# A round trip of queries and keys through DRAM, laid out by chunk and stack row

## The reference

```python
x = x + 0.5 * ffn(layernorm(x))      # gate and up 256 -> 2048, tanh-gelu(gate) * up, down 2048 -> 256
x = x + attention(layernorm(x))      # qkv = x @ w_project.T; softmax(q k / 4, causal) @ v; @ w_out.T
x = x + 0.5 * ffn(layernorm(x))
```

## Time and profile before

| | us |
|---|---|
| median of 3 runs | 1058.31 (1054.94 to 1059.23) |
| the profiled execution | 1055.69 |
| its span in the trace | 1053.6 |
| TensorE (PE) busy | 948.1 (90%) |
| VectorE (DVE) busy | 621.1 (59%) |
| ScalarE (ACT) busy | 469.9 (45%) |
| GpSimd (POOL) busy | 232.7 (22%) |
| DMA engines | 20.26 MB moved, 21803 packets |

### The profile page before, as it was taken

The page is one execution under the profiler, slowest core; times in us unless marked ns, Lnnn a source line. Parts: engine busy times, 40 slices in busy tenths (PEclk is TensorE's granted clock), DMA queues, the critical chain, the costliest instruction groups (busy, mean ns, idle before and its releaser), DMA issues.

```text
span 1053.6 us, 16739 instructions
## 1 busy us (share of the span) xinstructions
PE 948.1 (90%) x6726; PEld 410.9 (39%) x6726; DVE 621.1 (59%) x1008; ACT 469.9 (45%) x634; POOL 232.7 (22%) x261
## 2 busy tenths in 40 slices
PE   2879996998999999899999998999998685999998
PEld 1435553543444535224544222434322121255544
DVE  6986244654864688545788455688757574062221
ACT  2224142133227331796330998532298382933240
POOL 3744273033200440002330000042000000034140
PEclk9889998999999999999999999999999696999999
DMA  7000032006000060000230000000000000000000
GB/s 246 1 0 2 1 69 33 2 1 100 1 2 2 1 101 1 2 2 2 63 40 7 15 2 2 1 1 1 21 2 2 1 1 2 1 1 1 21 1 20
DMA packets 21803, 20.26 MB, mean 19 GB/s; under 512 B 4064, under 2 KB 21472, under 8 KB 21728
## 3 DMA queue, kind: packets, MB, share of 16 engines
q1 hardware_dynamic: 18528, 16.06, 7.9%
q10 hardware_dynamic: 3200, 3.15, 0.9%
HBM read 12.78 MB, written 6.29 MB: 18 GB/s over the span
## 4 chain that ended last, share of the span: by engine, by line
PE 74%; DVE 9%; ACT 6%; issue 5%; DMA 3%; SPq 1%; POOL 1%; ACTq 0%; DVEq 0%; POOLq 0%
PE ps L1102 11%; PE ps L1073 11%; PE ps L1074 10%; PE ps L1075 10%; PE ps L1251 10%; PE ps L1206 7%; PE ps L1103 5%; ACT inter L716 5%; PE ps L1234 5%; DVE sg L1011 2%; DVE sg L1014 2%; DMA qreg<-qk_split 2%; DVE oT L802 1%; PE ps L1218 1%; PE ps L1177 1%
## 5 line engine op out<-in xcount | busy, mean ns | idle before, releaser
L716 ACT ACTIVATE inter<-ps 128x1024 f32<-128x1024 f32 (+3 forms) x320 | 266.4, 899 | 65.9 <-PE ps L1234 51.6
L622 POOL TENSOR_TENSOR inter<-wreg,inter 128x512 f16<-128x512 f32 x112 | 129.5, 1158 | 690.4 <-ACT inter L705 690.2
L1014 DVE TENSOR_REDUCE sg<-ps 128x2 f32<-128x1024 f32 (+3 forms) x224 | 228.9, 1043 | 63.1 <-PE ps L1206 32.8
L726 ACT ACTIVATE wreg<-ps,gelu_in 128x512 f32<-128x512 f32 x112 | 77.1, 689 | 282.4 <-PE ps L1075 282.4
L1102 PE MATMUL ps<-wd,inter 128*128 128x512 f16 x512 | 171.0, 380 | 0.0
L1011 DVE TENSOR_REDUCE sg<-ps 128x1 f32<-128x512 f32 (+3 forms) x192 | 112.0, 628 | 95.5 <-PE ps L1206 64.4
L878 DVE SCALAR_TENSOR_TENSOR wreg<-ps,kappa,wreg 128x512 f32<-128x512 f32 x128 | 95.9, 749 | 106.8 <-PE ps L1075 103.9
L1251 PE MATMUL ps<-inter,v 128*17 128x512 f32 (+3 forms) x1280 | 155.6, 560 | 1.0
L1206 PE MATMUL ps<-kreg,qreg 48*128 48x512 f16 (+3 forms) x640 | 112.6, 364 | 35.7 <-DVE sg L1011 12.6
L1103 PE MATMUL ps<-wd,inter 128*128 128x256 f16 x512 | 139.6, 273 | 0.0
L1234 PE MATMUL ps<-qreg,kreg 50*128 50x512 f16 (+3 forms) x640 | 113.1, 366 | 25.8 <-ACT inter L716 14.4
(11 more groups left out here) (136 smaller groups left out, 903.6 us busy)
## 6 DMA issues: line engine op xcount, KB each, us to landing
qk_split<-oT SPq DMA_DIRECT2D x4, 1024.0 KB, 4.5
kreg<-qk_split SPq DMA_DIRECT2D x24, 128.0 KB, 4.6
qreg<-qk_split SPq DMA_DIRECT2D x24, 128.0 KB, 7.8
xres<-in_L_attn_x ACTq DMA_DIRECT2D x4, 512.0 KB, 9.0
out_x<-xres SPq DMA_DIRECT2D x4, 512.0 KB, 2.9
kreg<-in_L_ffn_up_W_packed ACTq DMA_DIRECT2D x4, 256.0 KB, 5.8
kreg<-in_L_ffn_gate_W_packed SPq DMA_DIRECT2D x4, 256.0 KB, 7.0
kreg<-in_L_ffn_down_W_packed SPq DMA_DIRECT2D x1, 1024.0 KB, 9.6
```

Source lines behind the costliest of these rows:

```text
L622: pool.tensor_tensor(inter[:, 1, u, :], prod_ring[:, u % 3, :], inter[:, 0, u, :], ALU.subtract).then_inc(s_inter, 1)
L716: act.activation(p_ring[:, pair % 8, :, 0:w], ps[:, 512 * b:512 * b + 1024].rearrange("p (a q) -> p a q", a=2)[:, :, 0:w], ACT.Exp, scale= ...
L1014: dve.tensor_reduce(m_part[:, r, part, col:col + 9:8], both[:, :, 0:width], AX.X, ALU.max).then_inc(s_slot_read, 1)
```

## The change

The DRAM tensor gets the shape [chunk, high or low, queries or keys, 32 stack rows, 8 pairs, 512 tokens], in which one stack row of one chunk is 8 KB in one piece. The key buffer gets the shape [chunk, pair, 512 tokens] in each partition, so that it takes such a row in one piece as well; the query buffers have that shape already. The one store of 1 MB becomes sixteen of 64 KB (2 x high or low, 2 x queries or keys, 4 x p), since the partition number of the source carries p, half and row mixed: each takes 32 partitions with 2 pieces of 1 KB. The six loads of keys and six of queries of each chunk remain, now with 16 pieces of 8 KB each. The waits on `s_qk_out` count 256 for a chunk in place of 16. The two products that read `kreg` (L1206, L1234) index it by chunk, pair and token within the chunk. The order of the work is the same.

```diff
-        kreg = sb("kreg", [P, NPAIR, T], f16)
+        kreg = sb("kreg", [P, NCH, NPAIR, CT], f16)
...
-        kflat = kreg[:, :, :].rearrange("p a t -> p (a t)").bitcast(i32)
+        kflat = kreg[:, :, :, :].rearrange("p c a t -> p (c a t)").bitcast(i32)
...
-        qk_dram = nc.dram_tensor("qk_split", [2, 4, P, T], f16, kind="Internal").ap()
+        qk_dram = nc.dram_tensor("qk_split", [NCH, 2, 2, 2 * HD, NPAIR, CT], f16, kind="Internal").ap()
...
-            def stack_source(c, m0, half, part):
-                return qk_dram[part, m0:m0 + 2, :, CT * c:CT * (c + 1)]\
-                    .rearrange("m (p a d) t -> a d (m p) t", a=2, d=HD)[half]
...
-                sp.dma_start(qk_dram[:, :, :, cols].rearrange("s m p t -> p s m t"), qk_flat).then_inc(s_qk_out, 16)
+                for part in range(2):
+                    for k in range(2):
+                        for p in range(4):
+                            sp.dma_start(qk_dram[c, part, k, :, :, :].rearrange("r (m p) t -> p r m t", p=4)[p],
+                                         qk_flat[32 * p:32 * p + 32, part, 2 * k:2 * k + 2, :])\
+                              .then_inc(s_qk_out, 16)
...
-                sp.wait_ge(s_qk_out, 16 * (c + 1))
+                sp.wait_ge(s_qk_out, 256 * (c + 1))
...
-                        sp.dma_start(kreg[r:r + HD, :, cols],
-                                     stack_source(c, 2, half, (0, 0, 1)[row])).then_inc(s_kstack[c], 16)
+                        sp.dma_start(kreg[r:r + HD, c, :, :],
+                                     qk_dram[c, (0, 0, 1)[row], 1, HD * half:HD * half + HD, :, :]).then_inc(s_kstack[c], 16)
...
-                                     stack_source(c, 0, half, (0, 1, 0)[row])).then_inc(s_qstack[c], 16)
+                                     qk_dram[c, (0, 1, 0)[row], 0, HD * half:HD * half + HD, :, :]).then_inc(s_qstack[c], 16)
...
-                act.wait_ge(s_qk_out, 16 * min(c + 2, NCH))
+                act.wait_ge(s_qk_out, 256 * min(c + 2, NCH))
...
-                        act.wait_ge(s_qk_out, 16 * n)
+                        act.wait_ge(s_qk_out, 256 * n)
...
-                        last = pe.matmul(bank(at[a], w), qreg[c % 2][rows, pair, q0:q0 + P], kreg[rows, pair, k0:k0 + w],
+                        last = pe.matmul(bank(at[a], w), qreg[c % 2][rows, pair, q0:q0 + P], kreg[rows, part, pair, 0:w],
...
-                    last = pe.matmul(dst[a], kreg[rows, pair, P * j:P * j + P], qreg[c % 2][rows, pair, q0:CT],
+                    last = pe.matmul(dst[a], kreg[rows, j // TPC, pair, P * (j % TPC):P * (j % TPC) + P], qreg[c % 2][rows, pair, q0:CT],
```

More of the change, by code:

```diff
@@ L460, in _ @@
                          w_out.rearrange("(m p) d -> p m d", p=P)).then_inc(s_out_in, 16)
-            def stack_source(c, m0, half, part):
-                return qk_dram[part, m0:m0 + 2, :, CT * c:CT * (c + 1)]\
-                    .rearrange("m (p a d) t -> a d (m p) t", a=2, d=HD)[half]
             def spread(c):
-                cols = slice(CT * c, CT * (c + 1))
                 sp.wait_ge(s_slot_read, place["qk", c])
-                sp.dma_start(qk_dram[:, :, :, cols].rearrange("s m p t -> p s m t"), qk_flat).then_inc(s_qk_out, 16)
+                for part in range(2):
[4 more added lines that the diff above has]
+                              .then_inc(s_qk_out, 16)
                 if c == 0:
                     sp.wait_ge(s_ones, 6)
-                sp.wait_ge(s_qk_out, 16 * (c + 1))
+                sp.wait_ge(s_qk_out, 256 * (c + 1))
                 for half in range(2):
```

## The result

The changed kernel takes 1068.58 us (median of 4 runs, 1067.33 to 1069.31), beside 1058.77 for the kernel before: a ratio of 1.0099 with a 95% interval of 1.0072 to 1.0125. A second comparison gave 1.010 (1.0069 to 1.013). It is slower by one per cent, some 10 us; 6 were forecast. The profiled execution took 1068.16 us with a span of 1066.0, 12.4 more than the span before and 2.6 more than the medians differ: the profiled execution before lies 3.1 us under its median.

What follows compares the result with a forecast made beforehand. TensorE was taken to bound the kernel, with transfers mattering only at its waits in chunks 0 and 1. Terms 0.7 + 4.45 + 0.85 = +6.0 us on the median 1058.3 gave 1064.3 us, range 1052 to 1070.

Steps and rivals of the forecast that it cites:

- The bound, and the two places: TensorE waits for the query stacks at L1206 in chunk 0 (7.91 us) and chunk 1 (4.38 us); each microsecond there counts.
- Loads unchanged, because 16 partitions and not 1 KB set 130 GB/s: Key and query loads stay at 14.1 and 13.8 us, since each still writes 16 partitions whatever the piece size.
- The price of a store's issue: On SP, 15 more store issues a chunk at a pitch of 0.47 us each (bounds 0.41 and 0.64).
- The landing of the last store: The last 64 KB store lands 1.8 us after its issue (bounds 1.4 and 3.1).
- Sum for chunk 1: Sixteen stores take 8.9 us against 4.46 for one: +4.45 us (+3.1 to +8.2).
- Chunk 0: Stores land at 152.9, the key buffer memset's 3.4 us of cover is used up, loads start 0.7 us later (0 to +4.5).
- The clock: TensorE's lower clock after its waits costs +0.85 us more in chunk 1 (0 to +0.85) and 0 in chunk 0.
- Cover of chunks 2 and 3: Loads there end 4.45 us later, hidden by other TensorE work, at no cost; chunk 2 has 25 us to spare.
- the case given 0.15: Rival of dearer loads or stores: stores at a pitch of 0.64 us give +13.6 us; chance 0.15.

Runs made afterwards that it cites:

- The run with one store: The changed kernel's layouts and 8 KB loads, but a single 1 MB store per chunk (queries and keys mixed up), against the kernel before: ratio 1.001.
- the test transfer: Kernel before plus, between key and query loads, 896 KB in 1 KB pieces sent into 112 partitions: landed in 5.3 us at 271 GB/s; kernel time not meaningful.
- the four stores: The changed kernel with the DRAM tensor reordered so four stores of 256 KB replace sixteen, loads still 8 KB pieces, against the kernel before: ratio 1.0004.
- the padded rows: The changed kernel with 64 unused columns behind each DRAM stack row, against the kernel before: ratio 1.0079, and 1.0047 run beside the changed kernel.
- the old layout: The kernel before with only its one store cut into sixteen of 64 KB, own DRAM tensor and 1 KB loads: ratio 1.0055, then 1.0045.
- the one with the first pairs first: The kernel before with its loads split, pairs 0 and 1 first, pairs 2 to 7 after: 1045.6 us, ratio 0.992.
- the joint comparison: Three kernels against the kernel before in one set: changed kernel 1.010, sixteen stores in its own old layout 1.0045, changed kernel with padded DRAM rows 1.0047.

## Why the prediction was right, and what in it was wrong

*The bound, and the two places* (step 1): right. TensorE waits for the query stacks in the same two places, and 11.9 us more there come out as 12.4 us of span.

*Loads unchanged, because 16 partitions and not 1 KB set 130 GB/s*: right, the step that decided the sign. 13.9 us in chunk 1 and 14.0 in chunk 0, against 14.1 and 13.8. The run with one store shows it with 8 KB pieces, the test transfer with 1 KB pieces, and the four stores point the same way in the other direction, at 32 partitions. The rule of the Trainium skill that the prediction set beside it (SBUF — State Buffer, "Door 1: The DMA port swizzle", bandwidth by the ports that the partitions reach) agrees with all three in order: 131 GB/s at 16 partitions, 183 to 235 at 32, 271 at 112. Its limit of 109 GB/s for 16 partitions is exceeded here by a fifth; but here several loads, into different groups of 16 partitions, are under way at once (issued every 0.47 us, landed in 2.9 us at the least), and no run shows the rate of one alone. That ports are the mechanism is its word; the runs show only that the rate goes with the number of partitions.

*The price of a store's issue*: wrong, and this is the failed step. The prediction had two rows for it, 0.47 us from the loads and 0.64 from the maxima's little DMAs, and took the first because the loads looked more alike in bytes. The pitch was 0.64, its upper bound. That is 15 x 0.17 = 2.6 us a chunk. What the padded rows show is that the pitch of the DRAM rows, just twice that of the pieces, makes these stores dear. That it does so because the two sides of the transfer are then cut unlike, 64 rows against 32, is argued and not shown. The four stores fit it (their DRAM side too is evenly spaced, 256 pieces against 32 partitions, and one issue takes 0.59 us at the least and 0.74 in the median), and so does the maxima's DMA, 2 partitions against 16, which wasn't tried. The changed kernel's loads show that an even pitch alone isn't dear: their 16 rows of 8 KB follow one another in DRAM without a gap, with the padding they don't, and the issue takes 0.42 us either way.

*The landing of the last store*, 1.8 us: 2.09 in the changed kernel and 1.76 with the cheap issue. Two readings beside it were off and moved nothing in the forecast: the lower bound should be 1.5 us and not 1.4 (64 KB are an eighth of the 512 KB), and chunk 0's store landed at 149.2 and not 148.8, since SP's wait of 4.8 us begins after the issue. Its cover was 3.0 us.

*Sum for chunk 1*, +4.45: it was +7.26. With 0.47 us an issue, in the old layout, it was 8.8 us against the 8.9 worked out, and 1.0045 to 1.0055 against 1.0057 (6.0 of 1058.3). So the mechanism holds, and with the cheap issue the total comes out; not each term does: in the first of these two runs chunk 0's loads started 1.7 us later and not 0.7, and chunk 1's took 15.0 us.

*Chunk 0*, +0.7: it was +4.6. Of the difference, 2.6 are the pitch, 0.3 the landing, and 1.0 that the first two issues of the kernel's first spread took longer; it appears in the old layout too (8.45 us for sixteen in chunk 0, 7.52 in chunk 1), no row of before could tell it, and its cause is open.

*The clock*, +0.85 for chunk 1 and 0 for chunk 0: 0.3 and 0.5. That the sum is the same is luck; chunk 1 didn't become like chunk 0, and chunk 0 lost more than before.

*Cover of chunks 2 and 3*: right, no wait of TensorE's there. The maxima rows behind chunk 2's spread had 8.2 us; they are now issued at 398.79, 1.3 us after SP is done with the spread at 397.51. It was nearly used up.

*The number*: 1064.3 was forecast and 1068.6 measured, inside the range of 1052 to 1070 but near its end. What came true is the case given 0.15, stores at a pitch of 0.64 with +13.6 us, in its mechanism, with loads as in the forecast. The forecast had the direction and the places right and one term of its sum, the issues, too small by a quarter (7.1 us for 15 pitches, 9.6 measured). Two rows gave two prices for an issue, and nothing in the rows of before told which of them fits; the case with the dearer one deserved more than a part of 0.15.

## What to carry to other kernels

Before making pieces larger, look for a transfer in the same trace with the same pieces that runs faster; here the store did, at 347 GB/s, and named the partition count as the bound. Price an added DMA by its issue on the queue, and where two rows give two prices, look at how the pieces lie on both sides and not only at their bytes; a small padding of the rows is a cheap trial. Where a transfer can't be made faster, ask what part of it the first reader needs: that gave 7 to 8 us where larger pieces cost 10.

## What the runs showed of the hardware beyond that

The same stores, byte for byte, cost SP 0.44 or 0.60 us each (medians) depending only on 128 bytes of padding behind each row in DRAM.

And much of the scatter between profiled executions arises in one place that none of these kernels changes, from the second store of the result to the third (attention 3 and a feed-forward stage). Stretches of equal work, granted clock in the third column from the end: the kernel before, the one with the first pairs first, and the padded one in the joint comparison.

```profile
756.60:988.00 231.40, 197.23 (x1483) 69.23 (x1484) 112.94 (x187) 136.11 (x166) 22.10 (x23) 0.90 0.01 3
```

```profile
746.90:981.00 234.10, 199.94 (x1483) 69.23 (x1484) 112.97 (x187) 136.16 (x166) 22.06 (x23) 0.89 0.01 3
```

```profile
760.20:987.70 227.50, 193.43 (x1483) 68.98 (x1484) 112.98 (x187) 135.84 (x166) 22.05 (x23) 0.92 0.01 3
```

227.5 to 234.1 us for the same instructions, with a granted clock of 0.92 to 0.89 in the mean. A single profiled execution can therefore be 7 us off another for no reason of the change, which is why the span of the padded kernel (1053.2 us) says nothing against its ratio, and why the faster kernel's span is only 7.1 us shorter although its two waits and the clock behind them give back about 10.
